# Dealing the row-maximum units of an attention stage from a table, and one mask matmul for four diagonal squares

## The chip, the cores and the metric

The kernel runs on one core of one Trainium2 chip. The metric is the device time of one execution in microseconds (us), as the median of several runs. TensorE is called PE in the profile (PEld is its weight load), VectorE is DVE, ScalarE is ACT, GpSimd is POOL, and SP is the engine that issues most transfers.

## The reference

The reference normalises x (4 batches of 1024 rows of 256), runs multi-head attention with a latent key and value of width 64 (16 heads of width 16, causal), normalises the result and adds it, and then does the same with a mixture of 8 experts of which 2 are taken. The part around the change is the attention:

```python
attn = jnp.einsum('bhtl,bsl->bhts', q_lat, c_kv) / math.sqrt(hs)
attn = jnp.where(causal_mask[None, None], -jnp.inf, attn)
attn = jax.nn.softmax(attn, axis=-1)
ctx = jnp.einsum('bhts,bsl->bhtl', attn, c_kv)
```

## The kernel before

The kernel has four stages one after the other: a projection, the attention (`attend`), the routing, and the experts. The change touches only `attend`.

The attention works on 16 groups of 4 heads each: 4 batches (`b`) by 4 groups (`g`). The first three batches are a hardware loop on PE, ACT, DVE and SP, and the last is written out. A group has 24 steps, numbered k = 0 to 23. A step is one block of scores for two heads: the keys of tile j against the 512 queries of half c. Half c = 0 has steps 0 to 7 (key tiles 0 to 3), half c = 1 has steps 8 to 23 (key tiles 0 to 7). A block is two steps, so a group has 12 blocks. On the diagonal only the queries at or after the keys are computed, so the scores are 512, 384, 256 and 128 queries wide in steps 0 to 7 and in steps 16 to 23, and 512 wide in steps 8 to 15.

The softmax needs the maximum of each row before the exponentials of the group begin. It is found one and two groups ahead, in 38 "units" for each group (`max_units`). A unit fills one PSUM bank of 512 floats with scores (rows on the partitions, keys along the bank), and DVE reduces it to one maximum for each row and head. Where a piece ends on the diagonal, a second matmul (identity by a matrix `future` that is very negative above the diagonal) adds the causal mask to its last 128 columns (line 657). Units 0 and 1 hold four diagonal squares each, and so four scores matmuls and four mask matmuls. There are three banks (`ps_m`), used in turn, so unit n waits until DVE has read unit n - 3 (`free`, semaphores `bank_read`). The same three banks serve three other jobs: `out` (PE transposes the output of a half, L672; ACT copies it to `sums`, L758), `turn` 0 (PE transposes the maxima, L666; ACT copies them, L745; SP sends them into the rows of q of the next group), and `turn` 1, which only takes a bank and gives it back.

The order on each engine is the order of the program. PE does, for every step: `scores` (L690, which waits for the exponential two steps back), then the jobs of the step, and in steps 1, 5, 9, ... 21 the `values` of two blocks (L707): in step 5 blocks 0 and 1, in step 9 blocks 2 and 3, and so on, in step 1 the last two of the group before. ACT does the exponential of each step (L772), then what the jobs of the step ask of it. POOL does, for each step: at step 8 `split` (four long instructions on a weight of the experts, L611 and L615), then for an `out` job `divide` (a power, L593, and a product, L595), and then, at the odd step that ends a diagonal block, `clear` (a select that sets the masked exponentials to zero, L603). `values` of a diagonal block wait for its `clear` (semaphore `masked`). Diagonal blocks are 0 to 3 and 8 to 11.

`bank_jobs` deals the jobs to the steps (table `AFTER`). Before, it does so by costs, and puts `out` 0 into step 5, `out` 1 into step 13 and the two `turn` jobs into step 16. The dealt order of one group is, as units for each step: steps 0 to 23 have 2, 0, 2, 2, 3, 0, 3, 3, 2, 0, 2, 1, 1, 0, 1, 1, 2, 0, 2, 2, 2, 0, 3 and 4 units. All of them stand before the values of their step, and steps 1, 5, 9, 13, 17 and 21 have none. In the last but one group only the 20 units of steps 0 to 11 are left (units 18 to 37 of the last group), in the last group none.

Of the kernel before, what the change touches and what calls it, by code (L numbers as in the profile page):

```python
# [1 line left out]

# [1 line left out]

# [10 lines left out]
P = 128  # L16
# [4 lines left out]
CH = 512  # L21
NCH = T // CH
TC = CH // P
# [355 lines left out]
STEPS = [(c, j, p) for c, j in BLOCKS for p in range(2)]  # L379
NB, NS = len(BLOCKS), len(STEPS)  # L380
# [27 lines left out]
UNITS = max_units()  # L408
NU = len(UNITS)
HALF = NU // 4 * 2  # L410
# [3 lines left out]
def unit_keys(m):  # L414
    heads, pieces = UNITS[m]
    return len(heads) * sum(keys for _, _, keys, _ in pieces)


MATMUL, VALUES, SWITCH, MASK = 0.235 / CH, 0.44 / CH, 0.2, 0.125


def past(k):

    c, j, _ = STEPS[k]
    return max(0, (j - c * TC) * P)


def bank_jobs():

    work = [("unit", 1, m) for m in range(HALF, NU)] + [("unit", 2, m) for m in range(HALF)]
    cost = [unit_keys(m) * MATMUL + len(UNITS[m][0]) * MASK * any(k0 + keys == (i + 1) * P for i, k0, keys, _ in UNITS[m][1])
            for _, _, m in work]
    taken = [2 * (CH - past(k)) * MATMUL for k in range(NS)]
    for k in range(1, NS, 4):
        taken[k] += SWITCH + sum((CH - past(2 * (blk % NB))) * VALUES for blk in (k // 2 - 2, k // 2 - 1))
    even = (sum(taken) + sum(cost)) / NS
    room = [max(0, even - t) for t in taken]
    out, step, done = [[] for _ in STEPS], 0, 0  # L440
    for job, c in zip(work, cost):
        while step < NS - 1 and (done + c / 2) / sum(cost) > sum(room[:step + 1]) / sum(room):
            step += 1
        out[step].append(job)
        done += c
    out[5] += [("out", 0, 0)]
    out[13] += [("out", 0, 1)]
    out[16] += [("turn", 1, 0), ("turn", 1, 1)]
    return out


AFTER = bank_jobs()
JOBS = sum(len(x) for x in AFTER)
assert JOBS % NBK == 0 and NB % NPT == 0


def attend(nc, d, keep, slots):
# [3 lines left out]
    with ExitStack() as ctx:  # L461
        s = Store(nc, ctx, "att")
        ident, identb, future = keep["ident"], keep["identb"], keep["future"]
        y = keep["y"]
        for g in range(1, NSL):
            add_slot(slots, s, g)
        qg, kg, vg, loaded = slots["q"], slots["k"], slots["v"], slots["loaded"]
# [29 lines left out]
        def ahead(b, g, n):  # L497

            return not isinstance(b, int) or b * NG + g + n < B * NG
# [5 lines left out]
        def numbered(b):  # L505


            out, n = [], len(first)
            for g in range(NG):
                steps = []  # L510
                for k in range(NS):
                    here = [j for j in AFTER[k] if ahead(b, g, j[1])]
                    steps.append([(j, n + i) for i, j in enumerate(here)])
                    n += len(here)
                out.append(steps)
            return out, n

# [4 lines left out]
        with nc.Block() as block:  # L522
# [109 lines left out]
            def _(pe):  # L632
# [10 lines left out]
                def unit(b, g, m, out):  # L643

                    heads, pieces = UNITS[m]
                    slot = g % NSL
                    if m == 0:
                        pe.wait_ge(loaded[slot], at(b, g // NSL * NSL, LOADS, NSL * LOADS + ONES))
                    end = 0
                    for i, k0, keys, _ in pieces:  # L650
                        for h in heads:
                            diag = k0 + keys == (i + 1) * P
                            ins = pe.matmul(out[:, end:end + keys], qg[slot][:, h // 2, i * P:(i + 1) * P],  # L653
                                            kg[slot][:, h, k0:k0 + keys], start=True, stop=not diag)
                            end += keys
                            if diag:
                                ins = pe.matmul(out[:, end - P:end], identb[:], future[:], start=False, stop=True)  # L657
                    return ins

                def max_turn(b, g, half, out):  # L660
# [14 lines left out]
                def jobs(b, g, todo):  # L675
                    for (kind, more, m), n in todo:
                        free(b, n)
                        do = {"unit": unit, "turn": max_turn, "out": turn_out}[kind]
                        do(b, g + more, m, ps_m[n % NBK]).then_inc(bank_made[n % NBK], 1)
# [33 lines left out]
                def body(b):  # L713
                    for g, steps in enumerate(numbered(b)[0]):
                        for k in range(NS):
                            scores(b, g, k)
                            jobs(b, g, steps[k])
                            if k % 4 == 1:
                                for blk in (k // 2 - 2, k // 2 - 1):
                                    if blk >= 0:  # L720
                                        values(b, g, blk)
                                    elif g > 0:
                                        values(b, g - 1, NB + blk)
                    for blk in (NB - 2, NB - 1):
                        values(b, NG - 1, blk)

# [954 lines left out]
```

## Time and profile before

| | us |
|---|---|
| median of 3 runs | 1468.88 (1466.34 to 1469.29) |
| the profiled execution | 1465.89 |
| its span, first to last instruction | 1464.2 |
| attention, first scores to the last group's end | 200.4 to about 782 |
| PE busy in the span | 1133.9 (77%) |

The profiled execution is 1.7 us longer than its span. Rows with a time and a duration are of the timeline, counted from the start of the span. A PE row with x4 merges four matmuls that follow each other; their ends are modelled and overlap the next start, so a pace is read from the distance of starts. PEclk is the granted clock of TensorE as a share of 2.4 GHz, so that 0.50 is 1.2 GHz.

### The profile page before, as it was taken

Reading aid. Unit: us, or ns where it says so; the run is one execution under the profiler, and the core shown is the slowest. Engines: PE = TensorE matmul, PEld = TensorE weight load, DVE = VectorE, ACT = ScalarE, POOL = GpSimd, SP = SyncE. Lnnn points to the kernel's source line nnn. Section 1 sums busy time; section 2 is a strip of 40 time slices with the busy share of each in tenths; the row PEclk is TensorE's granted clock in tenths of the full one; section 3 lists DMA queues with packets and bytes.
Section 4 is the critical chain, followed back from the end, with each engine's and each line's share of the span. In section 5 each row is a group of like instructions: output and inputs, shape, how many; then the busy total and the mean of one; then the engine's idle time right before and its main releaser. Section 6 shows DMA issues by size and latency. Waiting matters only on the chain. (4 is left out here: it accounts for less than half of the span.)

```text
span 1464.2 us, 26459 instructions
## 1 busy us (share of the span) xinstructions
PE 1133.9 (77%) x7809; PEld 840.9 (57%) x7810; DVE 806.4 (55%) x2033; ACT 650.0 (44%) x1112; POOL 596.2 (41%) x687
## 2 busy tenths in 40 slices
PE   5852759998999899999982533299999999999800
PEld 3421435554555455555531523299999999999800
DVE  5521646665666566666613863065555455555554
ACT  3430035554555455555573642144344344344443
POOL 4203135553555355555574677322222222222228
PEclk9985679999999999999996555599999999999955
DMA  4974223343333333343224413424324224231163
GB/s 148 288 196 147 83 94 128 141 140 142 121 142 138 143 123 141 140 144 122 88 88 142 173 70 119 162 94 162 103 102 161 98 103 165 78 120 43 47 233 115
DMA packets 95194, 189.88 MB, mean 130 GB/s; under 512 B 27940, under 2 KB 58932, under 8 KB 86868
## 3 DMA queue, kind: packets, MB, share of 16 engines
q1 hardware_dynamic: 87448, 166.92, 33.9%
q0 software_dynamic: 7680, 22.09, 4.3%
q8 instruction: 39, 0.64, 0.2%
q14 instruction: 27, 0.22, 0.1%
HBM read 109.44 MB, written 79.02 MB: 129 GB/s over the span
## 5 line engine op out<-in xcount | busy, mean ns | idle before, releaser
L772 ACT ACTIVATE att_pt<-att_ps_s 128x1024 f32<-128x1024 f32 (+3 forms) x384 | 305.0, 812 | 271.8 <-PE att_ps_s L690 269.4
L802 DVE TENSOR_REDUCE att_pm<-att_ps_m 128x1 f32<-128x512 f32 (+1 forms) x512 | 298.8, 650 | 145.6 <-PE att_ps_m L657 115.5
L1466 ACT ACTIVATE moe_hf<-moe_ps_h,moe_b 128x256 f32<-128x256 f32 x288 | 135.0, 474 | 241.7 <-PE moe_ps_h L1417 230.0
L653 PE MATMUL att_ps_m<-att_k,att_q 128*128 128x512 f32 (+3 forms) x576 | 202.5, 409 | 17.0 <-DMA att_v<-vs 9.3
L603 POOL TENSOR_SCALAR_AFFINE_SELECT att_pt<-att_pt 128x512 f32<-128x512 f32 x128 | 80.6, 635 | 291.1 <-ACT att_pt L772 291.1
L690 PE MATMUL att_ps_s<-att_q,att_k 128*128 128x512 f32 (+3 forms) x576 | 169.2, 378 | 12.4 <-ACT att_pt L772 6.3
L1386 POOL DMA_INDIRECT ys<-moe_o,moe_home x72 | 73.5, 1021 | 201.0 <-DVE moe_o L1498 190.0
L653 PEld LDWEIGHTS att_ps_m<-att_k,att_q 128*128 128x128 f32 x576 | 114.8, 202 | 58.3 <-DVE att_pm L802 43.6
L1492 DVE TENSOR_TENSOR moe_hTl<-moe_hf,moe_hTh 128x256 fp32r<-128x256 f32 x288 | 123.9, 430 | 9.9
L690 PEld LDWEIGHTS att_ps_s<-att_q,att_k 128*128 128x128 f32 x576 | 91.9, 191 | 64.0 <-issue 30.8
L657 PE MATMUL att_ps_m<-keep_future,keep_identb 128*128 128x128 bf16 x512 | 119.1, 240 | 0.0
L593 POOL TENSOR_TENSOR att_rec<-att_sums,att_minus 128x16 f32<-128x16 f32 x33 | 95.9, 2907 | 38.3 <-ACT att_sums L758 38.3
L1490 DVE CAST moe_hTh<-moe_hf 128x256 fp32r<-128x256 f32 x288 | 85.0, 295 | 47.8 <-ACT moe_hf L1466 44.4
L707 PE MATMUL att_ps_o<-att_pt,att_v 128*17 128x512 f32 (+3 forms) x1152 | 107.2, 489 | 1.8 <-POOL att_pt L603 1.8
L1417 PE MATMUL moe_ps_h<-moe_xTh,weights_w_0h 128*128 128x256 f32 x288 | 84.4, 293 | 13.3 <-issue 10.3
L1498 DVE TENSOR_TENSOR moe_o<-moe_ps_o,moe_b 128x256 f32<-128x256 f32 x72 | 27.2, 420 | 110.0 <-PE moe_ps_o L1428 110.0
L1417 PE MATMUL moe_ps_h<-moe_xTl,weights_w_0h 128*128 128x256 f32 x288 | 83.8, 291 | 0.0
L1417 PE MATMUL moe_ps_h<-moe_xTh,weights_w_0l 128*128 128x256 f32 x288 | 83.8, 291 | 0.0
L1417 PE MATMUL moe_ps_h<-moe_xTh,moe_w1h 128*128 128x256 f32 x288 | 81.3, 282 | 2.5 <-PE moe_ps_o L1428 2.5
L690 PE MATMUL att_ps_s<-slots_q,slots_k 128*128 128x512 f32 (+3 forms) x192 | 60.5, 401 | 28.6 <-DMA slots_q<-att_mt 16.2
L1428 PE MATMUL moe_ps_o<-weights_w_0h,moe_hTh 128*128 128x256 f32 x288 | 82.0, 285 | 0.0
L1428 PE MATMUL moe_ps_o<-moe_w2h,moe_hTh 128*128 128x256 f32 x288 | 82.0, 285 | 0.0
(188 smaller groups left out, 2588.7 us busy)
## 6 DMA issues: line engine op xcount, KB each, us to landing
att_raw<-in_w SPq DMA_DIRECT2D x16, 1024.0 KB, 5.7
ws<-att_raw_hi SPq DMA_DIRECT2D x16, 1024.0 KB, 5.1
ws<-att_raw SPq DMA_DIRECT2D x16, 1024.0 KB, 6.8
moe_rows<-xs SPq DMA_DIRECT2D x38, 258.0 KB
weights_w_0h<-ws SPq DMA_DIRECT2D x8, 1024.0 KB
weights_w_0l<-ws SPq DMA_DIRECT2D x8, 1024.0 KB
att_q<-qs SPq DMA_DIRECT2D x48, 128.0 KB
att_k<-ks SPq DMA_DIRECT2D x48, 128.0 KB
```

Source lines behind the costliest of these rows:

```text
L593: pool.tensor_tensor(rec[:, c], got[:, :, :, HS], minus[:], ALU.pow).then_inc(rec_done, 1)
L653: ins = pe.matmul(out[:, end:end + keys], qg[slot][:, h // 2, i * P:(i + 1) * P], kg[slot][:, h, k0:k0 + keys], start=True, stop=not diag)
L657: ins = pe.matmul(out[:, end - P:end], identb[:], future[:], start=False, stop=True)
L690: ins = pe.matmul(out[:, e, off:CH], kg[slot][:, 2 * p + e, j * P:(j + 1) * P], qg[slot][:, p, c * CH + off:(c + 1) * CH], start=True, sto ...
L707: ins = pe.matmul(ps_o[32 * h:32 * h + VW, off:CH], vg[slot][:, j, h * VW:(h + 1) * VW], pt[:, blk % NPT, h, off:CH], start=(j == 0), stop ...
L772: act.activation(pt[:, blk % NPT, 2 * p:2 * p + 2, off:CH], ps_s[k % 2][:, :, off:CH], ACT.Exp, scale=HS ** -0.5).then_inc(ex_done, 1)
L802: return dve.tensor_reduce(pm[:, g % 2, place, h:h + 1], src, AX.X, ALU.max)
L1417: ins = pe.matmul(ps_h[f % NHB][:], w1[r][a][:, k, f * P:(f + 1) * P], xT[m][:, k], start=(n == 0), stop=(n == 3 * CT - 1))
L1428: ins = pe.matmul(ps_o[t][:], hT[a][:, f, t * P:(t + 1) * P], w2[r][m][:, f], start=(f == 0 and (a, m) == pieces[0]), stop=(f == FT - 1 an ...
L1466: act.activation(hf[:, f % NHB], ps_h[f % NHB][:], ACT.Relu, bias=b1[r][:, f:f + 1]).then_inc(hf_done, 1)
L1490: dve.tensor_copy(hT[0][:, f], hf[:, f % NHB]).then_inc(hh_done, 1)
L1492: dve.tensor_tensor(hT[1][:, f], hf[:, f % NHB], hT[0][:, f], ALU.subtract).then_inc(hl_done, 1)
```

## The change

There are three edits, all in `attend` and in the table that it works from.

- `bank_jobs` no longer works from costs. A table `DEALT` gives for each step how many units come before the values of the step ("early") and how many after them ("late"). The largest number in one stretch is 3 (late in step 9), else 2.
- `out` 0 moves from step 5 to step 7, `out` 1 from step 13 to step 15, the two `turn` jobs from step 16 to step 17. They stand at the end of the early jobs of their step.
- A unit whose pieces are all diagonal squares (units 0 and 1) first gets one mask matmul over the whole bank, 512 columns wide (`future` repeated four times by its access pattern), and then four scores matmuls that add to it.

```diff
-MATMUL, VALUES, SWITCH, MASK = 0.235 / CH, 0.44 / CH, 0.2, 0.125
...
+DEALT = ((1, 0), (1, 2), (1, 0), (2, 0), (2, 0), (1, 0), (2, 0), (0, 0), (2, 0), (1, 3), (1, 0), (2, 0),
+         (2, 0), (2, 0), (0, 0), (2, 0), (2, 0), (1, 0), (1, 0), (1, 0), (2, 0), (1, 1), (0, 0), (2, 0))
...
-    out[5] += [("out", 0, 0)]
-    out[13] += [("out", 0, 1)]
-    out[16] += [("turn", 1, 0), ("turn", 1, 1)]
+    work = iter([("unit", 1, m) for m in range(HALF, NU)] + [("unit", 2, m) for m in range(HALF)])
+    out = []
+    for k, (early, late) in enumerate(DEALT):
+        extra = {7: [("out", 0, 0)], 15: [("out", 0, 1)], 17: [("turn", 1, 0), ("turn", 1, 1)]}.get(k, [])
+        out.append((list(islice(work, early)) + extra, list(islice(work, late))))
...
-                    end = 0
-                    for i, k0, keys, _ in pieces:
-                        for h in heads:
-                            diag = k0 + keys == (i + 1) * P
-                            ins = pe.matmul(out[:, end:end + keys], qg[slot][:, h // 2, i * P:(i + 1) * P],
-                                            kg[slot][:, h, k0:k0 + keys], start=True, stop=not diag)
-                            end += keys
-                            if diag:
-                                ins = pe.matmul(out[:, end - P:end], identb[:], future[:], start=False, stop=True)
+                    pieces_of = [(i, k0, keys, h) for i, k0, keys, _ in pieces for h in heads]
+                    squares = len(pieces_of)
+                    whole = all(keys == P and k0 == i * P for i, k0, keys, _ in pieces_of)
+                    if whole:
+                        pe.matmul(out[:, 0:squares * P].rearrange("p (s k) -> p s k", k=P), identb[:],
+                                  future[:].unsqueeze(1).to_broadcast([P, squares, P]), start=True, stop=False)
+                    for n, (i, k0, keys, h) in enumerate(pieces_of):
+                        diag = k0 + keys == (i + 1) * P and not whole
+                        end = (n + 1) * keys
+                        ins = pe.matmul(out[:, end - keys:end], qg[slot][:, h // 2, i * P:(i + 1) * P],
+                                        kg[slot][:, h, k0:k0 + keys], start=not whole,
+                                        stop=not diag and (not whole or n == squares - 1))
+                        if diag:
+                            ins = pe.matmul(out[:, end - P:end], identb[:], future[:], start=False, stop=True)
...
-                            jobs(b, g, steps[k])
+                            jobs(b, g, steps[k][:steps[k].early])
                             if k % 4 == 1:
...
+                            jobs(b, g, steps[k][steps[k].early:])
```

The class `Step` is a list with the number of its early jobs; ACT, POOL and DVE go through early and late jobs alike, in the numbered order, as before.

## Rows read from the trace of the kernel before

**Rows 1.** Page, part 1: busy us, share of the span, instructions.

```profile
PE 1133.9 (77%) x7809; PEld 840.9 (57%) x7810; DVE 806.4 (55%) x2033; ACT 650.0 (44%) x1112; POOL 596.2 (41%) x687
```

**Rows 2.** Windows: length, then busy us of PE, PEld, DVE, ACT, POOL, clock, DMA.

```profile
320.00:454.00 134.00, 124.72 (x826) 70.98 (x826) 83.14 (x144) 75.05 (x103) 69.38 (x59) 0.97 0.36 128
```

**Rows 3.** Timeline of PE: the scores of step 0 in six groups (start, us, what).

```profile
502.41 0.79 PE L690 MATMUL att_ps_s<-slots_q,slots_k 128*128 128x512 f32 x1 [4.93 <-issue]
...
540.18 0.40 PE L690 MATMUL att_ps_s<-att_q,att_k 128*128 128x512 f32 x1
...
576.28 0.40 PE L690 MATMUL att_ps_s<-att_q,att_k 128*128 128x512 f32 x1
...
612.39 0.39 PE L690 MATMUL att_ps_s<-att_q,att_k 128*128 128x512 f32 x1
...
720.26 0.63 PE L690 MATMUL att_ps_s<-att_q,att_k 128*128 128x512 f32 x2
...
751.28 0.47 PE L690 MATMUL att_ps_s<-att_q,att_k 128*128 128x512 f32 x1 [0.34 <-ACT att_pt L772]
```

**Rows 4.** Waits of the group at 576.3 to 612.4: total us, times, longest.

```profile
PEld att_ps_m L653 <- DVE att_pm L802: 3.7, 10, 0.4
...
PE att_ps_s L690 <- ACTq L740: 0.6, 1, 0.6
```

**Rows 5.** Waits of the last but one group, 720.3 to 751.3.

```profile
PEld att_ps_m L653 <- DVE att_pm L802: 2.2, 6, 0.4
```

**Rows 6.** Timeline: DVE in steps 22 and 23, and two units of PE in step 19.

```profile
573.40 4.28 DVE L802 TENSOR_REDUCE att_pm<-att_ps_m 128x1 f32<-128x512 f32 x7 [1.59 <-PE att_ps_m L657]
...
580.58 0.63 PE L653 MATMUL att_ps_m<-att_k,att_q 128*128 128x512 f32 x2
```

**Rows 7.** Timeline of one group, steps 5 to 9: PE and POOL.

```profile
583.11 0.65 PE L672 MATMUL att_ps_m<-keep_ident,att_ot 128*128 128x128 f32 x4
...
584.36 2.91 POOL L593 TENSOR_TENSOR att_rec<-att_sums,att_minus 128x16 f32<-128x16 f32 x1 [2.06 <-ACT att_sums L758]
...
587.92 1.22 POOL L603 TENSOR_SCALAR_AFFINE_SELECT att_pt<-att_pt 128x512 f32<-128x512 f32 x2
...
589.86 0.84 PE L707 MATMUL att_ps_o<-att_pt,att_v 128*17 128x256 f32 x16
```

**Rows 8.** Timeline of the last group, steps 5 to 9: PE and POOL.

```profile
756.25 0.60 PE L672 MATMUL att_ps_m<-keep_ident,att_ot 128*128 128x128 f32 x4
...
758.41 0.66 PE L690 MATMUL att_ps_s<-att_q,att_k 128*128 128x128 f32 x4
...
760.97 1.22 POOL L603 TENSOR_SCALAR_AFFINE_SELECT att_pt<-att_pt 128x512 f32<-128x512 f32 x2
...
761.66 1.00 PE L707 MATMUL att_ps_o<-att_pt,att_v 128*17 128x256 f32 x16 [1.15 <-POOL att_pt L603]
```

**Rows 9.** Timeline of PE in unit 0 (two of four masks), and four transposes.

```profile
557.17 0.23 PE L657 MATMUL att_ps_m<-keep_future,keep_identb 128*128 128x128 bf16 x1
...
557.36 0.23 PE L657 MATMUL att_ps_m<-keep_future,keep_identb 128*128 128x128 bf16 x1
...
558.44 0.60 PE L672 MATMUL att_ps_m<-keep_ident,att_ot 128*128 128x128 f32 x4
```

**Rows 10.** Windows at the half clock and beside a wait; columns as in rows 2.

```profile
502.00:508.60 6.60, 6.19 (x19) 5.05 (x20) 2.67 (x4) 3.38 (x5) 0.63 (x1) 0.50 0.28 88
755.00:775.00 20.00, 15.75 (x104) 6.96 (x103) 0.00 (x0) 13.46 (x20) 16.11 (x12) 1.00 0.42 156
```

**Rows 11.** PE after two waits in the experts' stage, and the windows behind them.

```profile
1056.36 0.38 PE L1417 MATMUL moe_ps_h<-moe_xTh,weights_w_0h 128*128 128x256 f32 x1 [3.44 <-issue]
...
1278.11 0.58 PE L1417 MATMUL moe_ps_h<-moe_xTh,weights_w_0h 128*128 128x256 f32 x1 [3.43 <-issue]
...
1056.00:1059.00 3.00, 2.64 (x22) 2.64 (x23) 1.05 (x4) 1.16 (x3) 0.85 (x1) 1.00 1.01 404
...
1277.00:1284.00 7.00, 5.89 (x29) 5.90 (x30) 2.16 (x6) 1.81 (x4) 1.30 (x2) 0.54 0.95 376
```

More of the change, by code:

```diff
@@ L2 @@
 from contextlib import ExitStack
+from itertools import islice
 import numpy as np
@@ L416, in unit_keys @@
     return len(heads) * sum(keys for _, _, keys, _ in pieces)
-MATMUL, VALUES, SWITCH, MASK = 0.235 / CH, 0.44 / CH, 0.2, 0.125
-def past(k):
-    c, j, _ = STEPS[k]
-    return max(0, (j - c * TC) * P)
+DEALT = ((1, 0), (1, 2), (1, 0), (2, 0), (2, 0), (1, 0), (2, 0), (0, 0), (2, 0), (1, 3), (1, 0), (2, 0),
+         (2, 0), (2, 0), (0, 0), (2, 0), (2, 0), (1, 0), (1, 0), (1, 0), (2, 0), (1, 1), (0, 0), (2, 0))
+assert sum(map(sum, DEALT)) == NU
 def bank_jobs():
[L432 to L445, printed above, removed]
-    out[5] += [("out", 0, 0)]
-    out[13] += [("out", 0, 1)]
-    out[16] += [("turn", 1, 0), ("turn", 1, 1)]
-    return out
+    work = iter([("unit", 1, m) for m in range(HALF, NU)] + [("unit", 2, m) for m in range(HALF)])
[3 more added lines that the diff above has]
+        out.append((list(islice(work, early)) + extra, list(islice(work, late))))
+    return out
+class Step(list):
+    early = 0
 AFTER = bank_jobs()
-JOBS = sum(len(x) for x in AFTER)
+JOBS = sum(len(x) + len(y) for x, y in AFTER)
 assert JOBS % NBK == 0 and NB % NPT == 0
@@ L511, in numbered @@
                 for k in range(NS):
-                    here = [j for j in AFTER[k] if ahead(b, g, j[1])]
-                    steps.append([(j, n + i) for i, j in enumerate(here)])
-                    n += len(here)
+                    early, late = ([j for j in part if ahead(b, g, j[1])] for part in AFTER[k])
+                    steps.append(Step((j, n + i) for i, j in enumerate(early + late)))
+                    steps[-1].early = len(early)
+                    n += len(steps[-1])
                 out.append(steps)
```

## The prediction

> **What bounds the kernel now.** I read the page first for the shares: PE is the busiest engine of the span, but with 77% no bound by itself [rows 1]. The windows say more: the change lies wholly in the attention, and in a stretch of it PE is busy for 124.7 of 134 us, DVE for 62%, ACT for 56% and POOL for 52% [rows 2]. So the attention goes at the pace of PE, and whatever makes PE wait is on the path. Starts of step 0 give the period: 612.39 - 576.28 = 36.11 us for a full group, 37.77 us for the group after a loop turn, 31.02 us for the last but one [rows 3]. The last group ends at about 782.
>
> Next I read what PE waits for in one period. It waits for DVE to give banks back: 3.7 us in ten waits, and 0.6 us behind the `turn` jobs, where `turn` 1 wants the bank of a unit that was only just made [rows 4]. The waits come where the table puts units back to back: DVE takes seven in 4.28 us, one every 0.60 us [rows 6], while PE makes an unmasked one in 0.23 us (two take 0.63 by the row, one alone 0.40) [rows 3, 6].
>
> The third view is the timeline of POOL around an `out` job. The transposes of `out` 0 begin at 583.11; the power begins at 584.36 and takes 2.91; the two selects that follow the division begin at 587.92 and take 1.22, so they end at 589.14; `values` of blocks 2 and 3, which need them, begin at 589.86 [rows 7]. So the selects are ready 0.7 us before they are wanted. In the last group, which has no units to fill steps 6 to 8, they are not: PE stands idle for 1.15 us, and the idle time is ended by POOL's select [rows 8].
>
> **The change part by part. 1. Fewer waits for banks: gain.** A step with two units costs DVE 1.20 us, and PE about 0.46 for scores and 0.46 to 0.7 for units. By the new table two double steps stand side by side in three places (3 and 4, 12 and 13, 15 and 16), and each leaves a debt to DVE of some 0.3 us, of which three banks absorb part; the three late units of step 9 find three free banks. I put 0.5 us for banks, 0.4 for `turn` 1 (unit 8's reduction, now with unit 9 made in between), and 0.4 for waits on exponentials, which come nearer when PE goes faster: 1.3 us. Before it was 3.7 + 0.6 = 4.3. Gain 3.0 us for each full group. The bounds: nothing left at all (4.3), and half left (2.1).
>
> **2. One mask for four: a small gain.** In unit 0 the masks start 0.19 us apart [rows 9], so the unit costs 4 x 0.19 = 0.75. Four transposes of 128 columns take 0.60, of which the last's own length is 0.27, so 0.11 each [rows 9]; a 128-column scores matmul behind another I take at the same. No row shows a bf16 mask of 512 columns. Its nearest row is the 512-column unit, 0.23 [rows 6]. Then the unit costs 0.23 + 0.44 = 0.67, a gain of 0.08, and 0.16 for the two. From above, a mask now costs 0.19 - 0.11 = 0.08 beyond its square and four of them 0.32, and a wide one might be paid on top of a full reload, 0.40: that is a loss of 0.09 for the unit. So -0.16 to +0.18 for each group; I take -0.15. The Trainium skill (TensorE: Matmul & The Clock Gate, Back-to-back issue gap) has a matmul cost its columns at the clock plus a fixed 2.5 ns, which speaks against this edit: four masks of 128 would cost 0.22 us and one of 512 0.216. By it the gain would be nothing, by the rows 0.15 us for each group; the kernel's own spacing of 0.19 for a 128-column pair is far over the page's [rows 9].
>
> **3. `out` 0 two steps later: loss.** ACT, POOL and PE do the same work for it, only later, and `values` of block 3 stays in step 9. From the first transpose at T, the power begins at T + 1.25 and the first select at T + 4.81 [rows 7]. In the new order the select of block 2 stands ahead of the division (step 5), and only that of block 3 behind it, so block 3 is free at T + 4.81 + 0.64 = T + 5.45 (a select is half of 1.22 plus the overlap, 0.64). What PE has to do between T and block 3: the transposes and the change to the next kind 0.48; step 8, two scores and two units, 4 x 0.23 = 0.92; step 9, two scores and one unit, 0.69, and 0.10 to switch; block 2, half of the pair's 0.84, 0.43. Sum 2.62. PE waits 2.85 us for each group. Behind the waiting `values` are queued the three late units, the scores of step 10 and ACT's copy of the first half's output in step 10, so DVE and ACT run dry too and nothing hides it. Before, the cover was the work of steps 5 (values of two blocks), 6, 7 and 8, some 6.7 us from 583.11 to 589.86 [rows 7]; that cover is what the edit gives up. Bounds: 2.4 (ACT is idle and copies at once) and 3.3.
>
> The rest costs nothing: `out` 1 in step 15 has its select in step 17 and its reader in step 21; the `turn` in step 17 has seven steps before the next group, over 10 us, for SP's four small transfers; SP's load of the group three ahead and its expert weights are queued behind that and shift by under 1 us; POOL's `split` begins after the select of block 3, 3 us later, and POOL is half idle [rows 2].
>
> **Sum.** A full group: -3.0 - 0.15 + 2.85 = -0.3 us, for 14 groups -4.2. In the last but one group the units gone are those of the second half; waits were 2.2 [rows 5], I let 0.4 remain: -1.8 + 2.85 = +1.0. In the last group PE already waits for the selects; `out` 0 slides from 756.25 behind the values of step 5 and step 6 to behind the scores of 758.41, some 2.4 us, less the 0.3 us that its own transposes spare the steps before: +2.1 [rows 8]. Together -1.1 us.
>
> **4. The clock.** The waits of before are short and spread over the group; now most of the idle time is one wait of nearly 3 us in each group. What the rows show of such waits: after 4.93 us of idle PE the granted clock is 0.50 for the 6.6 us that follow (1.2 GHz), and the group is 37.77 - 36.11 = 1.66 us longer [rows 3, 10]. After 3.44 us it stayed at full level once, and after 3.43 us it fell to 1.2 GHz for most of 7 us [rows 11]. With a wait of 1.15 us it stayed full [rows 8, 10]. 2.85 is nearer 3.4 than 1.15; PE's work on both sides (transposes before, units paced by DVE) is thin. I take a fall in ten of the 16 groups. One costs between 1.66 us (steps 0 to 4, where ACT's exponentials hide part) and, with PE the only bound, half of 6.6, 3.3 us; a stretch half as long costs half of that. I take 1.4. That makes +14. Bounds: no falls 0; a fall in each group at 2 us, +32.
>
> Total: -1.1 + 14 = +13 us on an execution of 1465.9, that is 1479. The median of the runs shown stands 3 us above the profiled one, so +13 on 1468.9: **1482 us**.
>
> **The rivals.** *The clock stays up.* For it: one 3.4 us wait left it alone [rows 11], and these are shorter. Then only the sum counts: 1468.9 - 1.1 = 1467.8, with the bounds of parts 1 to 3 some 1460 to 1475. *The even dealing gives more than I count (the other side).* One mechanism: my step costs add up to 35.5 us for a group of 36.1, so 0.6 us is lost to weight loads that show where unit follows unit; spread units may hide them, and the clock stays up. 15 x (0.3 + 0.6) = 13.5, less 3 for the last two groups: 1458. It decides in favour of faster as soon as the mask wait is under 2.5 us and the clock holds. *Every group falls.* 16 x 1.4 to 2.0 us: about +27, 1495. The Trainium skill (TensorE: Matmul & The Clock Gate, HAM oscillation) tells of a kernel that waited once in each tile of its loop and started every tile at the low clock. By that rule it is this rival and not my ten of 16; the 3.44 us wait that left the clock alone speaks against it [rows 11].
>
> **Chances.** My forecast 0.60, clock stays up 0.20, more gained 0.12, every group falls 0.08. The forecast's own range is 1472 to 1490. For 8 in 10 I go down to 1461, which takes in the middle of the second case, and up to 1491. This kernel's runs differ by 0.2%, 2.9 us, which is the least that can be told from none: faster is the third case and nearly half of the second, 0.20; within it the rest of the second and the low edge of the first, 0.15; slower 0.65.
>
> **What would show it.** Right: in step 9 of each group the first `values` matmul of block 3 idle for 2 to 3 us, ended by POOL's L603; PE's waits on L802 in a period down from 3.7 us to under 1; clock digits under 9 in the attention's slices; a period of 35.8 us where the clock holds and 37 or more where it does not. Wrong: no idle time there (I misread POOL's order), the clock at 1.00 all through, or many waits on L802 left.

## The result and the profile after

The changed kernel takes 1488.18 us (median of 4 runs, 1485.91 to 1488.5) and the kernel before 1469.09 us (1466.34 to 1470.85) on the same chip: a ratio of 1.0128, with a 95% interval of 1.011 to 1.0147. That is 19 us slower, where the forecast was 13 us slower.

Its profiled execution has a span of 1484.2 us, 20.0 us more than before. The page of after, part 1 and the row of the clock in part 2, looks almost as it did [rows 1]:

```profile
PE 1123.6 (76%) x7713; PEld 843.6 (57%) x7714; DVE 811.9 (55%) x2033; ACT 641.2 (43%) x1112; POOL 594.0 (40%) x687
...
PEclk9975679999999999999997555599999999999955
```

PE has 96 matmuls fewer and is busy 10 us less in a longer span, so PE has more idle time. Where it is, the starts of step 0 tell. From the first scores to the last step of the last group the attention took 578.3 us before and takes 596.1 after (199.8 to 795.9); the rest of the span went from 885.9 to 888.1. So 17.9 of the 20.0 us are in the attention. The timeline of after, PE, step 0 of five groups (start, us, what), answers to [rows 3]:

```profile
395.59 0.48 PE L684 MATMUL att_ps_s<-att_q,att_k 128*128 128x512 f32 x1
...
432.16 0.48 PE L684 MATMUL att_ps_s<-att_q,att_k 128*128 128x512 f32 x1
...
468.96 0.48 PE L684 MATMUL att_ps_s<-att_q,att_k 128*128 128x512 f32 x1
...
732.01 0.46 PE L684 MATMUL att_ps_s<-att_q,att_k 128*128 128x512 f32 x1
...
765.70 0.47 PE L684 MATMUL att_ps_s<-att_q,att_k 128*128 128x512 f32 x1 [0.34 <-ACT att_pt L767]
```

The two full groups between the first three rows take 36.57 and 36.80 us instead of 36.11 (others of the loop, away from its turns, up to 38.5), the last but one 33.70 instead of 31.02. What PE waits for in the group of 36.57, from the waits of after between 395.6 and 432.2 (total us, times, longest), answers to [rows 4]:

```profile
PE att_ps_o L701 <- POOL att_pt L592: 2.8, 1, 2.8
...
PEld att_ps_m L647 <- DVE att_pm L792: 1.1, 1, 1.1
...
PE att_ps_m L647 <- DVE att_pm L792: 1.0, 1, 1.0
...
PEld att_ps_m L647 <- DVE att_pm L797: 0.3, 1, 0.3
```

L797 is DVE's reduction of a unit with rows of one head (L802 before): the wait for it fell from 3.7 us to 0.3. L592 is `clear`: the wait of step 9. And there are 1.0 us for a bank that DVE gives back at L792, its reduction of units 0 and 1 (PEld and PE name the same stretch). Two stretches of the timeline, all engines, show them. First a group whose clock stays up:

```profile
286.77 2.90 POOL L582 TENSOR_TENSOR att_rec<-att_sums,att_minus 128x16 f32<-128x16 f32 x1 [2.78 <-ACT att_sums L753]
...
289.76 0.62 POOL L584 TENSOR_TENSOR keep_y<-att_sums,att_rec 128x256 f32<-128x256 f32 x1
...
290.33 0.64 POOL L592 TENSOR_SCALAR_AFFINE_SELECT att_pt<-att_pt 128x512 f32<-128x512 f32 x1
...
291.02 0.41 PE L701 MATMUL att_ps_o<-att_pt,att_v 128*17 128x128 f32 x8 [2.65 <-POOL att_pt L592]
...
291.90 3.08 DVE L797 TENSOR_REDUCE att_pm<-att_ps_m 128x1 f32<-128x512 f32 x5 [3.10 <-PE att_ps_m L647]
...
292.91 4.71 POOL L604 TENSOR_TENSOR att_raw<-att_raw,att_raw_hi 128x1024 fp32r<-128x1024 f32 x2
...
295.50 2.15 DVE L805 TENSOR_TENSOR att_pm<-att_pm 128x16 f32<-128x16 f32 x1
...
297.58 0.68 DVE L792 TENSOR_REDUCE att_pm<-att_ps_m 128x4 f32<-128x512 f32 x1
...
298.31 0.44 PE L647 MATMUL att_ps_m<-slots_k,slots_q 128*128 128x384 f32 x1 [0.96 <-DVE att_pm L792]
```

The power, the product and one select of POOL run from 286.77 to 290.97, and `values` of block 3 start at 291.02 after 2.65 us idle. That is the step 9 wait as forecast. Then comes what was not: DVE's small maximum of the job `negate` (L805), two inputs of 16 columns, takes 2.15 us. It ends at 297.65, and POOL's second long subtraction of `split` ends at 292.91 + 4.71 = 297.62. The reduction of L792 stands behind it, and PE, which wants that bank, is idle for 0.96 us. DVE's five reductions before it, partly beside the same subtractions, kept their pace of 0.62 us. The next is the group before it, in which the clock fell:

```profile
252.80 0.63 PE L701 MATMUL att_ps_o<-att_pt,att_v 128*17 128x128 f32 x8 [2.95 <-POOL att_pt L592]
...
254.69 4.71 POOL L604 TENSOR_TENSOR att_raw<-att_raw,att_raw_hi 128x1024 fp32r<-128x1024 f32 x2
...
260.11 0.17 DVE L805 TENSOR_TENSOR att_pm<-att_pm 128x16 f32<-128x16 f32 x1
```

Here PE's work came later, the subtractions were over at 259.40, and the same maximum took 0.17 us. The windows of after (length, busy us of PE, PEld, DVE, ACT, POOL, then clock and DMA) for that fall, for a stretch with the wait and no fall, and for the two parts of the kernel, answer to [rows 2, 10]:

```profile
252.40:259.20 6.80, 6.40 (x26) 3.84 (x26) 3.30 (x5) 2.46 (x3) 6.80 (x5) 0.50 0.22 72
...
291.00:305.00 14.00, 12.97 (x88) 7.91 (x92) 10.70 (x18) 8.01 (x10) 7.96 (x5) 1.00 0.21 74
...
200.00:796.00 596.00, 531.98 (x3500) 306.52 (x3501) 353.33 (x597) 320.55 (x461) 298.48 (x255) 0.95 0.35 125
796.00:1484.00 688.00, 482.57 (x3865) 475.44 (x3864) 373.20 (x1245) 278.78 (x568) 255.63 (x389) 0.81 0.34 119
```

The granted clock was 0.50 (1.2 GHz) for 6.8 us from 252.4, right behind the wait. Such a stretch stands behind the step 9 wait in 11 of the 16 groups, of 3.4 us in eight and of 6.8 us in three. In the five others the clock stayed up, and there step 13 takes 4.38 us instead of 3.22.

### The profile page after: what moved, and what is told of

Same layout as the page of the kernel before. It is cut to its first block and busy times, and to the rows that moved or that the text cites. A ratio compares the mean times of both kernels' runs of the same rounds, so it can differ in the third digit from the quotient of the medians.

```text
span 1484.2 us, 26267 instructions
## 1 busy us (share of the span) xinstructions
PE 1123.6 (76%) x7713; PEld 843.6 (57%) x7714; DVE 811.9 (55%) x2033; ACT 641.2 (43%) x1112; POOL 594.0 (40%) x687
## 5 line engine op out<-in xcount | busy, mean ns | idle before, releaser
L767 ACT ACTIVATE att_pt<-att_ps_s 128x1024 f32<-128x1024 f32 (+3 forms) x384 | 298.0, 813 | 296.9 <-PE att_ps_s L684 293.6
L797 DVE TENSOR_REDUCE att_pm<-att_ps_m 128x1 f32<-128x512 f32 (+1 forms) x512 | 309.8, 651 | 207.2 <-PE att_ps_m L647 103.7
L647 PE MATMUL att_ps_m<-att_k,att_q 128*128 128x512 f32 (+3 forms) x576 | 195.7, 409 | 4.8 <-DVE att_pm L792 3.8
L684 PE MATMUL att_ps_s<-att_q,att_k 128*128 128x512 f32 (+3 forms) x576 | 172.2, 390 | 5.0 <-ACT att_pt L767 4.8
L592 POOL TENSOR_SCALAR_AFFINE_SELECT att_pt<-att_pt 128x512 f32<-128x512 f32 x128 | 81.3, 635 | 200.1 <-ACT att_pt L767 200.1
L1381 POOL DMA_INDIRECT ys<-moe_o,moe_home x72 | 73.7, 1024 | 204.7 <-DVE moe_o L1493 193.7
L701 PE MATMUL att_ps_o<-att_pt,att_v 128*17 128x512 f32 (+3 forms) x1152 | 111.6, 496 | 34.7 <-POOL att_pt L592 34.1
L684 PEld LDWEIGHTS att_ps_s<-att_q,att_k 128*128 128x128 f32 x576 | 95.0, 199 | 54.2 <-issue 28.1
L651 PE MATMUL att_ps_m<-keep_future,keep_identb 128*128 128x128 bf16 x384 | 95.0, 247 | 0.0
L1412 PE MATMUL moe_ps_h<-moe_xTh,moe_w1l 128*128 128x256 f32 x288 | 80.9, 281 | 0.0
```

Of the source, the lines that this page charges most:

```text
L647: ins = pe.matmul(out[:, end - keys:end], qg[slot][:, h // 2, i * P:(i + 1) * P], kg[slot][:, h, k0:k0 + keys], start=not whole, stop=not ...
L684: ins = pe.matmul(out[:, e, off:CH], kg[slot][:, 2 * p + e, j * P:(j + 1) * P], qg[slot][:, p, c * CH + off:(c + 1) * CH], start=True, sto ...
L701: ins = pe.matmul(ps_o[32 * h:32 * h + VW, off:CH], vg[slot][:, j, h * VW:(h + 1) * VW], pt[:, blk % NPT, h, off:CH], start=(j == 0), stop ...
L767: act.activation(pt[:, blk % NPT, 2 * p:2 * p + 2, off:CH], ps_s[k % 2][:, :, off:CH], ACT.Exp, scale=HS ** -0.5).then_inc(ex_done, 1)
L797: return dve.tensor_reduce(pm[:, g % 2, place, h:h + 1], src, AX.X, ALU.max)
L1412: ins = pe.matmul(ps_h[f % NHB][:], w1[r][a][:, k, f * P:(f + 1) * P], xT[m][:, k], start=(n == 0), stop=(n == 3 * CT - 1))
```

## The experiments

Two theories follow from this profile. By the first, step 9's wait and the clock behind it are the loss. By its rival, the loss is DVE's maximum held by POOL's subtractions, and the falls of the clock cost less than they seem to because they keep the two apart. The runs were made on several chips, so each ratio is to the kernel before on its own chip, with the 95% interval, and times of different chips are compared by these ratios. The lengths of groups and steps are of the one profiled execution of each kernel.

**Take away the wait: `out` 0 back in step 5.** After, with

```diff
-        extra = {7: [("out", 0, 0)], 15: [("out", 0, 1)], 17: ...
+        extra = {5: [("out", 0, 0)], 15: [("out", 0, 1)], 17: ...
```

> The changed kernel with one edit undone: the first out job is dealt to step 5 again. Theory 1 (the select of block 3 stands behind the division, and PE waits for it in step 9): the 2.66 us of idle PE in each of 16 groups go, but not wholly, since step 5 now lies only 4.2 us of PE work ahead of block 2's values and the chain takes 4.8 to 5.5; about 0.6 us stays. The period of a full group without a fall of the clock goes from 36.6 to about 34.3, the clock no longer falls in the groups, and the kernel takes about 1445 us (1435 to 1455). Rival (the dealt order itself makes PE slower, and the idle time would turn up in another step): the kernel stays over 1469.

1449.08 us, 0.9883 [0.9851, 0.9915]. Step 9 takes 3.11 us (5.39 after) and the clock stays up in the groups. In the waits from 380 to 480 the 2.8 us for the select are gone:

```profile
PE att_ps_o L701 <- POOL att_pt L592: 1.1, 3, 0.4
```

Step 13 is now 4.4 us in all groups but the last two, and there DVE's maximum takes 2.17 to 2.19 us. So one line of the table carries the whole loss, some 36 us by the ratios, and the held maximum costs less than what the rest of the change brings.

**Take away the wait otherwise: the select before the division.** After, with POOL's `clear` ahead of `divide` in the step:

```diff
+                            if k % 2 == 1 and k // 2 in DIAG:
+                                clear(b, g, k // 2)
                             for what, n in step:
...
-                            if k % 2 == 1 and k // 2 in DIAG:
-                                clear(b, g, k // 2)
```

> The changed kernel with GpSimd's order turned round within a step: the select first, then the division; the table is untouched and the first out job stays in step 7. Theory 1: the wait in step 9 goes completely, 16 times 2.7 to 2.9 us, and with it the falls of the clock, so about 1438 us (1428 to 1448), a little under the run with the job in step 5. Rival (the wait is for something else that comes last in step 9, such as the exponential of block 3): 1480 or more.

1444.42 us, 0.9841 [0.9808, 0.9874], 6 us over the expected 1438. Its timeline, POOL, PE and SP's queue:

```profile
572.69 0.64 POOL L592 TENSOR_SCALAR_AFFINE_SELECT att_pt<-att_pt 128x512 f32<-128x512 f32 x1 [2.22 <-ACT att_pt L767]
...
573.29 2.90 POOL L582 TENSOR_TENSOR att_rec<-att_sums,att_minus 128x16 f32<-128x16 f32 x1
...
574.23 0.84 PE L701 MATMUL att_ps_o<-att_pt,att_v 128*17 128x256 f32 x16
...
589.19 2.70 SPq L520 DMA_DIRECT2D att_q<-att_mt  x4
...
597.37 0.72 PE L684 MATMUL att_ps_s<-att_q,att_k 128*128 128x512 f32 x2 [1.04 <-DMA att_q<-att_mt]
```

`values` start without a wait, while the division runs. A new wait shows at the end of the group: step 0 of the next group waits for SP's four small transfers of the row maxima, issued from 589.19 and wanted at 596.3. The `turn` in step 17, which I had priced at nothing with "over 10 us" to spare, is late once the group is shorter. The 10 us were misread already: in the changed kernel steps 17 to 23 take 8.9 us, and from the issue of the first transfer to step 0 there are 6.9 (11.3 in the kernel before).

**Keep the wait, keep PE busy in it.** After, with nine matmuls of 512 columns into a scores bank whose last reader is done:

```diff
+                    if blk == 3:
+                        pe.wait_ge(ex_done, at(b, g, NS, 11))
+                        for _ in range(9):
+                            pe.matmul(ps_s[0][:, 0, :]..., identb[:], future[:]..., start=True, stop=True)
```

> The changed kernel with nine more matmuls (512 columns of bf16, into a scores bank that is free at that time and overwritten by the next scores) just ahead of the wait for the select of block 3, so that PE works through some 2 us of the wait. The output is unchanged. Theory as predicted (each of the 11 falls of the clock in the groups costs 1.4 us): the granted clock stays at full in all groups and the time falls by some 12 to 15 us, to about 1474. Rival, from the trace of the changed kernel (a group without a fall loses 1.2 us in step 13, where DVE's small product waits for GpSimd's long subtraction, and a group with a fall does not): the clock stays up but step 13 takes 4.4 us in all groups, so the gain is half or less, 1480 to 1488.

1473.88 us (10 runs), 1.0050 [1.0030, 1.0071]. The timeline of PE, and the window of fourteen groups:

```profile
251.25 2.12 PE L695 MATMUL att_ps_s<-keep_future,keep_identb 128*128 128x512 bf16 x9
...
254.27 0.41 PE L706 MATMUL att_ps_o<-att_pt,att_v 128*17 128x128 f32 x8 [0.90 <-POOL att_pt L592]
```

```profile
238.00:760.00 522.00, 488.88 (x3274) 279.07 (x3274) 342.79 (x559) 281.28 (x409) 262.95 (x225) 0.99 0.37 130
```

The idle time before `values` of block 3 is 0.90 us in place of 2.95 in this group, 0.6 in most; step 9 is as long as in the changed kernel (5.39), and no fall follows it in any group (two falls remain, at turns of the loop, where before has them too). The time is as the clock's term had it, but the rival's mark is there too: step 13 takes 4.39 us in all groups but the last two. Both are real, and the clock is worth 0.78% net, 11.5 us.

**The step's move in the kernel before.** Before, with `out[5] += [("out", 0, 0)]` written as `out[7] +=`.

> The kernel before with one part of the change alone: the first out job is dealt to step 7 in place of step 5. Theory 1: the wait for the select of block 3 comes in each group, 2.7 to 2.9 us, with falls of the clock in part of them, and nothing is gained in exchange: 16 times 2.8 is 45 us, with the clock some 1510 to 1525. Rival (the old order has more units between the job and the values of block 3, so the cover holds): within 3 us of 1469.

1532.4 us, 1.0442 [1.041, 1.0474]: 65 us slower, more than expected. Waits from 380 to 480:

```profile
PE att_ps_o L707 <- POOL att_pt L603: 8.1, 3, 2.8
```

The wait is the same 2.7 us, but a full group (622.1 to 662.6) takes 40.46 us in place of 36.11: step 9 is 2.85 us longer, steps 10 to 12 are 1.47 longer at the lower clock, which falls behind this wait in 14 of the 16 groups, and steps 5 and 7 are 0.14 longer between them. Without the even dealing the same move costs its full price.

**Put the two mends together: `turn` in step 14.** The second experiment's kernel, with `17: [("turn", ...` written as `14: [("turn", ...`.

> The run with the select first, and the two turn jobs moved from step 17 to step 14. Theory 2 (with the wait in step 9 gone, the group is so short that the rows of maxima, which SP sends after the turn job and which take some 8 us to arrive, come last at step 0 of the next group): the extra 1.1 to 2.9 us at the end of eight groups, 15 us in all, go, to about 1428 us. Rival (the transfer is slow because of its place in SP's queue behind the loads of a group, not because it is asked for late): 1440 or more.

1440.16 us, 0.9796 [0.9765, 0.9828]: 4 us gained (7 by the ratios) where some 16 were expected. That is the rival's number but not its mechanism, since the wait for the row maxima nearly went (windows of waits 530 to 700, the second experiment first, then this one):

```profile
PE att_ps_s L684 <- DMA att_q<-att_mt: 5.9, 3, 2.7
```

```profile
PE att_ps_s L684 <- DMA att_q<-att_mt: 0.7, 1, 0.7
```

but steps 14 and 15 now take 0.98 + 1.73 us instead of 0.57 + 1.37, 0.8 us more in each group, which eats most of the gain.

**Take away the subtractions.** The kernel just told, with POOL's subtractions left out:

```diff
-                        pool.tensor_tensor(raw[:, part].bitcast(F32R), raw[:, part], raw_hi[:, part], ALU.subtract
-                                           ).then_inc(split_lo, 1)
+                        pool.nop().then_inc(split_lo, 1)
```

> The run with the turn jobs in step 14, and GpSimd's two long subtractions of the split (2.4 us each, once a group) left out, so that the low halves of the experts' weights are not computed; all else is the same. Theory 3 (DVE's small maximum of two tiles, 0.17 us by itself, is held until GpSimd's running subtraction ends, and PE waits for a bank behind it in step 13): that instruction falls from 2.2 to about 0.2 us, step 13 from 4.3 to 3.2 us, 14 times 1.1 is 15 us less than the run it is made from. Rival (step 13 is long for its own work, the first block of the second half with its wait for ScalarE's copy): no change over 3 us.

1436.49 us, 0.977 [0.974, 0.98]. By groups of instructions from 230 to 690 (count, busy us, mean ns), DVE's maximum with the subtractions and without:

```profile
L805 DVE TENSOR_TENSOR att_pm<-att_pm 128x16 f32<-128x16 f32 x13 | 27.8, 2139 | 0.0
```

```profile
L804 DVE TENSOR_TENSOR att_pm<-att_pm 128x16 f32<-128x16 f32 x13 | 2.1, 162 | 0.0
```

This shows who holds it: 2.14 us fall to 0.16, and step 13 from 4.4 to 3.21. But the time fell by 4 us and not by the 15 expected, since PE reached the end of the group sooner than the row maxima did: step 23, 0.74 us without a wait, took 1.1 to 4.5 us in most groups. Behind three of these waits the clock fell to 0.50 for 3.4 us (from 409.9, 553.2 and 659.0), which it did nowhere away from the loop's turns in the kernel this one is made from.

**The division behind the split.** The kernel with `turn` in step 14, where at step 8 POOL first does `split` and then the division of `out` 0; everything is computed.

> The run with the turn jobs in step 14, and on GpSimd the division of the first out job put behind the split instead of ahead of it, so that the subtractions run 3.6 us earlier and are over when DVE comes to its small maximum; nothing is left out. Theory 3: as with the subtractions left out, some 10 to 15 us less than the run it is made from, about 1413 to 1418 us, the best so far. Rival (any long instruction of GpSimd on two tiles holds DVE's, so that the power takes the place of the subtraction): the small maximum still takes over 1 us and the time is that of the run it is made from.

1435.28 us, 0.9774 [0.9753, 0.9796], the fastest with all of the work in it: 2.3% under before and some 52 us under the change, but 5 us gained where 10 to 15 were expected. DVE's maximum takes half:

```profile
L808 DVE TENSOR_TENSOR att_pm<-att_pm 128x16 f32<-128x16 f32 x13 | 15.1, 1162 | 0.0
```

It is still held by the subtractions, which now end sooner but not soon enough. The timelines of POOL and of DVE in one group:

```profile
564.36 4.74 POOL L604 TENSOR_TENSOR att_raw<-att_raw,att_raw_hi 128x1024 fp32r<-128x1024 f32 x2
...
568.22 0.91 DVE L808 TENSOR_TENSOR att_pm<-att_pm 128x16 f32<-128x16 f32 x1
```

The subtractions end at 569.10 and the maximum at 569.13. In nine of the first fourteen groups it takes 0.9 us, and step 13 takes 3.22 as without subtractions; in the five others it takes 1.4 to 1.7 us. So neither the theory (the maximum would meet no subtraction) nor the rival (the power would hold it) came as written.

What is left is the end of the group, where PE waits for the row maxima: step 23 takes 1.3 to 3.3 us in seven groups away from the loop's turns. Where PE waited, the four transfers took 11.1 to 13.1 us from the first issue to their use, against 8.1 to 9.7 in the second experiment; why they take longer stays open. SP's queue has them (L520), the two stores of 1 MB right behind, and the next fetch 11 us later, when the stores have landed:

```profile
574.13 3.37 SPq L520 DMA_DIRECT2D att_q<-att_mt  x4
577.79 0.77 SPq L544 DMA_DIRECT2D ws<-att_raw_hi  x1
578.86 0.96 SPq L545 DMA_DIRECT2D ws<-att_raw  x1
...
591.21 0.41 SPq L537 DMA_DIRECT2D att_raw<-in_w  x1
```

**Four masks again.** That kernel with `whole = False`.

> The run with the division behind the split, with one edit of the change undone: units 0 and 1 get four mask matmuls each again. By the prediction one wide mask saves 0.08 us for a unit, 0.15 for a group, so this run is 2.3 us slower than the one it is made from. Rival by the plain stream times (four masks of 128 columns stream as long as one of 512): no difference.

1434.98 us, 0.9773 [0.9739, 0.9806]: no difference. The two steps with units 0 and 1 took 1.57 and 1.69 us instead of 1.47 and 1.60, so the wide mask spares 0.19 us for each group, as its term says (0.15), but this kernel waits at the end of the group and gives it back there. The waits for the row maxima from 235 to 690, with one mask and with four:

```profile
PE att_ps_s L687 <- DMA att_q<-att_mt: 7.5, 6, 2.2
```

```profile
PE att_ps_s L687 <- DMA att_q<-att_mt: 7.4, 6, 2.6
```

**The dealing alone.** After, with `out` in steps 5 and 13, `turn` in 16, and four masks.

> One part of the change alone: the table of units with its early and late jobs, but the out jobs in steps 5 and 13, the turn jobs in step 16, and four masks for units 0 and 1. By the prediction's term the dealing saves some 3 us of PE's waits in each of 14 groups, 42 us, and 1.8 in the next; against it stand what the other runs showed, 0.6 us in step 9 (less cover for the division) and 1.1 us in step 13 (DVE's small maximum held by GpSimd's subtraction). So about 14 times 1.3 is 18 us less than the kernel before, some 1450. Rival (the dealing gains only together with the jobs moved to steps 15 and 17): within 3 us of the kernel before.

1461.58 us, 0.9949 [0.9931, 0.9967]: 8 us gained where some 19 were expected. Step 13 takes 5.1 us, since `out` 1 and the held maximum now meet in it, and step 16 takes 1.85 with the `turn`. Its timeline:

```profile
401.48 1.00 PE L701 MATMUL att_ps_o<-att_pt,att_v 128*17 128x256 f32 x16 [0.36 <-POOL att_pt L592]
...
409.38 0.44 PE L647 MATMUL att_ps_m<-att_k,att_q 128*128 128x384 f32 x1 [0.79 <-DVE att_pm L792]
```

So the new steps of `out` 1 and `turn` and the wide mask together are worth the difference to the first experiment, some 10 us by the ratios (0.9949 and 0.9883). The held maximum costs more here than the 1.1 us counted: step 13 is 2.2 us longer than before.

**The select first, in the kernel before.**

> The kernel before, with GpSimd's select ahead of the division in each step, as a control. There the selects are ready 0.7 us before PE wants them in all groups but the last: gain of 1.4 us in the last group alone, so within 3 us of 1468. Rival (the order of GpSimd costs the kernel before something too): over 10 us less.

1468.51 us (10 runs), 1.0 [0.9983, 1.0017]. Nothing, as expected: the selects were in time [rows 7]. In the last group 0.3 us came of the 1.4 expected; PE still waits 0.90 us for the select there.

**Stores on POOL's queue.** The fastest kernel, with the stores of `split` and the next fetch issued by POOL, to free SP's queue for the row maxima.

> The run with the division behind the split, with the two stores of the split weights and the fetch of the next ones issued from GpSimd's queue, right behind the split and in step 22, in place of SP's. Theory 4 (with the other waits gone SP's own queue is the bound: loads of a group, the rows of maxima, two stores and the wait of some 13 us for their landing add up to 35 us for a group of 33): the waits of 1 to 3 us at the end of nine groups go, some 15 us, to about 1420. Rival (the transfers share the DMA engines, and the rows arrive late whoever issues the stores, or GpSimd is now late with its selects): no gain or a loss.

1457.58 us, 0.9921 [0.9898, 0.9945], some 22 us slower than with SP. The row maxima landed later, not sooner; the waits for them from 235 to 690 doubled (7.5 us before this edit):

```profile
PE att_ps_s L690 <- DMA att_q<-att_mt: 14.7, 6, 3.9
```

From the first issue to their use they took 12.0 to 14.6 us where PE waited. And with four of these waits the clock fell, three times for 6.8 us and once for 3.4, where the kernel with SP's stores has none away from the loop's turns. The window of one fall:

```profile
417.40:424.20 6.80, 5.59 (x28) 3.38 (x29) 1.50 (x3) 2.05 (x2) 0.63 (x1) 0.50 0.19 71
```

The stores start earlier here. Whether they slow the small transfers because both move at once, or through POOL's own issuing, was not taken apart.

**Busy PE and no subtractions.** The third experiment's kernel without the subtractions, so that the clock stays up and nothing holds DVE.

> The changed kernel with the nine matmuls in the wait of step 9 (the clock stays up in all groups), and GpSimd's two subtractions of the split left out, so that the low halves of the experts' weights are not computed. Theory 3, that the hold of DVE's small maximum is the term missing from the prediction: step 13 falls from 4.4 to 3.2 us in 14 groups, 15 us less than the run with the nine matmuls alone, about 1459 us; what is left of the attention is then the predicted 35.4 to 35.8 us for a full group. Rival (the hold is real but another wait, such as the rows of maxima at the end of the group, takes its place, as in the run without subtractions of the faster version): under 8 us less.

1461.14 us (10 runs), 0.9963 [0.9945, 0.9981]: some 13 us under the third by the ratios, 15 expected. The full groups of the loop, away from its turns, take 35.4 to 35.9 us, the one from 419.70 takes 35.41. DVE's maximum in the third and here, groups from 230 to 690:

```profile
L810 DVE TENSOR_TENSOR att_pm<-att_pm 128x16 f32<-128x16 f32 x12 | 26.1, 2177 | 0.0
```

```profile
L809 DVE TENSOR_TENSOR att_pm<-att_pm 128x16 f32<-128x16 f32 x12 | 2.0, 168 | 0.0
```

## Why the prediction was right, and what it lacked

The last run takes the attention apart, by its length in each profiled execution:

| | attention, us | step | ratio, all runs |
|---|---|---|---|
| before | 578.3 | | 1 |
| change, PE kept busy, no subtractions | 568.5 | -9.8: dealing, mask, step 9 wait, and the loop's turns | 0.9963 |
| change, PE kept busy | 586.7 | +18.2: DVE's maximum held in nearly all groups | 1.0050 |
| change | 596.1 | +9.4: the clock, less the holds that it spares | 1.0128 |

With +2.2 for the rest of the kernel that is the 20.0 us. The rest took 883 to 893 us in the profiled executions of all these kernels, so its 2.2 need not be the change's.

The steps of the table hold more than their names. At two turns of the hardware loop PE waits for something that the profile doesn't show: 10.0 us in sum before, 6.9 in the run without subtractions, 7.6 in the third experiment, 9.2 after, and the falls of the clock there differ in length too. Some 4 of the -9.8, 2 of the +18.2 and 1.6 of the +9.4 lie there. The profiled execution without subtractions was also the fastest of its ten, 8 us under their median. The change itself is thus worth about -5.5 without falls and holds, the holds +16, the clock +8 net; by the ratios of all runs the same steps are -5.4, +12.8 and +11.5.

**Fewer waits for banks** and **one mask**: predicted -3.0 and -0.15 for a full group. In the run without falls and holds a full group away from the turns is 0.2 to 0.8 us shorter than before, 0.55 in the mean, and with 2.66 us of step 9 wait in it the two are worth -3.2. Right within 0.1. The gain over the attention was still larger than I had put, about -5.5 in place of -1.1: a full group gains 0.55 in place of 0.3, and the last two lose 2.6 in place of 3.1. No run tests the mechanism of the rival with the larger gain, the weight loads. The mask's share was measured, 0.19 us for a group. The formula that I held against it from the Trainium skill (TensorE: Matmul & The Clock Gate, Back-to-back issue gap) is there that of an isolated matmul, and the page says itself that it counts too little at few columns; I had left that out.

**The step 9 wait**: predicted 2.85, measured 2.57 to 2.95 in the full groups, 2.65 typical; in the last group 3.22. Right, by the steps of the working: the select waited for the power and the product, and with the select put first the wait went.

**The clock**: predicted ten falls at 1.4 us, +14. There were eleven. Their net cost is 9.4 - 1.6 = 7.8 us in the attention. Nine of the groups with a fall were spared the hold, 1.17 us (step 13 3.22 against 4.39), so gross they cost (7.8 + 10.5) / 11 = 1.7 us each, some 18 in all. Against the same groups of the third experiment, and with the hold that they were spared, the falls of 3.4 us in full groups away from the turns cost 1.4 to 1.6 us, and the one of 6.8 us in the group from 237.54 cost 2.9: the price of 1.4 was right for a short fall, and I had none of the long ones in the groups. That the count came near is luck: ten was a guess between none and all, worked out from no row, and in the fourth experiment waits of the same length were followed by a fall in 14 of 16 groups. The rival of every group falling did not come, and neither did that of none. Waits of one length are followed by a fall in one group and by none in another (2.66 us at 447.13 and at 526.41 of the changed kernel); which it will be I can't tell from the rows, and it stays open. The Trainium skill (TensorE: Matmul & The Clock Gate, HAM oscillation) has a kernel that starts each tile at the low clock after one wait in each; the trace agrees for 11 groups of 16.

**What the sum lacked**: the held maximum. "A unit costs DVE 0.60 us" and "three banks absorb part" looked at DVE's reductions only, and I never asked how long its other instructions took, or beside what they ran. The trace of before had the answer in its groups (230 to 690):

```profile
L810 DVE TENSOR_TENSOR att_pm<-att_pm 128x16 f32<-128x16 f32 x12 | 13.8, 1147 | 0.0
```

A maximum of 16 columns at 1.15 us, seven times the 0.17 of the first one (ahead of the groups), was already held. The timelines of POOL and of DVE in the kernel before:

```profile
591.08 4.74 POOL L615 TENSOR_TENSOR att_raw<-att_raw,att_raw_hi 128x1024 fp32r<-128x1024 f32 x2
...
594.69 1.15 DVE L810 TENSOR_TENSOR att_pm<-att_pm 128x16 f32<-128x16 f32 x1
```

The subtractions end at 595.82, the maximum at 595.84. The pause there was shorter and PE did not wait for it; the new order brings the maximum just behind the start of the second subtraction, so it is held for 2.15 of that one's 2.36 us, and the bank is wanted at once. The Trainium skill (SBUF — State Buffer, SBUF: two separate sides) states such a lock: a DVE instruction with two SBUF inputs and a GpSimd instruction that reads SBUF share a port pair, and the later blocks until the first is done. The trace agrees, and so do those of all the kernels with subtractions: each maximum that begins while one runs, whether it takes 0.2 or 2.2 us, ends 0.03 to 0.04 us after it. The runs without subtractions agree too (0.16 and 0.17 us). So the +13 was near the 20 of the spans partly because errors offset: some 4.5 us of gain over the attention were missed, and against that stand the hold in the five groups without a fall (5 x 1.17 = 5.9), falls priced 4 too low, and 2.2 in the rest of the kernel. These come to 7.6 where 7 us were missing, which is as near as such a sum can be trusted.

**The signs**: step 9's wait, its release by POOL's select, and the fall of the bank waits came as written. The period of 35.8 us where the clock holds did not: in the loop, away from its turns, it is 36.6 to 36.8, since there the maximum is held, and 35.4 to 35.9 without the hold. Where the clock fell there it was 36.8 to 38.5. Clock digits under 9 in the attention did not: a slice of the page is 1484.2 / 40 = 37 us long, and a fall of 3.4 or 6.8 us leaves a mean of 0.95 or 0.91 in it. The windows show it; the page's digits are too coarse. And "the rest costs nothing" held only as long as the wait was there: with it gone, the `turn` in step 17 cost up to 2.7 us for a group.

## What to carry to other kernels

Before a job is moved on one engine, follow what it makes late on the engine that orders by program: here the division stood in front of a select that had nothing to do with it, and swapping the two turned a loss of 1.3% into a gain of 1.6%. In a trace, look at the mean of every group of instructions against its shortest: a tiny instruction that takes seven times its own length is held by something, and a new order can make that hold longer. And when a wait is taken away, see what arrives next in time, as the row maxima did here: leaving out the subtractions gave 4 us of 15, since that wait stood right behind. And a job that is moved brings its cost along: the `turn` in step 14 took away one wait and gave back 0.8 us in each group.

## What the runs showed of the hardware

- A DVE maximum of two 128x16 inputs took 0.16 to 0.17 us alone and 2.1 to 2.2 us beside POOL's fp32 subtraction of 1024 columns (2.36 us). Whenever it began while one ran it ended 0.03 to 0.04 us after it, in every trace. Reductions from PSUM beside the same subtractions kept 0.62 us each.
- A PE wait of 2.6 to 3.2 us was followed by 3.4 or 6.8 us at 1.2 GHz in 11 of 16 groups of the changed kernel and in 14 of 16 of the fourth experiment, and in none when nine matmuls filled 2.12 us of it. One fall cost about 1.7 us of the period, 1.4 to 1.6 where it lasted 3.4 us.
- The four transfers of row maxima, 8 KB each, were waited for until 8.2 us after the first was issued (589.19 to 597.37, the second experiment), and until 12.3 us after it in the fastest kernel (574.13 to 586.42).
